# A two-layer attention and state-space kernel: y kept in PSUM, and the products of a step in another order

## The reference, cut to what matters

```
scores  = einsum('bcihn,bcjhn->bcijh', Cc, Bc) * Ldec * dtc      # Ldec = masked exp(cum_i - cum_j)
y_intra = einsum('bcijh,bcjhp->bcihp', scores, xc)
states  = einsum('bcjh,bcjhn,bcjhp->bchpn', dtc * dlast, Bc, xc)
y_inter = einsum('bcihn,bchpn->bcihp', Cc * exp(cum), prev)
y = y_intra + y_inter + Dp * x
```

## Time and profile before

| | us |
|---|---|
| median of 3 runs | 2378.64 |
| the profiled execution, its own time | 2379.2 |
| its span (first to last instruction) | 2377.5 |
| PE busy | 2070.7 (87%) |
| DVE busy | 1677.6 (71%) |
| ACT busy | 1429.3 (60%) |
| POOL busy | 1341.0 (56%) |
| mean granted TensorE clock | 0.948 of full speed |

### The profile page before, as it was taken

How to read it: one execution, slowest core, us unless ns; L and a number is a source line. 1 busy time by engine, 2 the same in 40 slices (tenths; PEclk the granted TensorE clock), 3 DMA queues, 4 the chain that set the end, 5 groups by cost and what they waited for, 6 DMA issues and landing times.

```text
span 2377.5 us, 33832 instructions
## 1 busy us (share of the span) xinstructions
PE 2070.7 (87%) x11288; PEld 1573.5 (66%) x11288; DVE 1677.6 (71%) x2927; ACT 1429.3 (60%) x2692; POOL 1341.0 (56%) x1233
## 2 busy tenths in 40 slices
PE   8899886888988888888888888888888888988768
PEld 4666664666666676667666766666666666766545
DVE  5777564667866787678667866786678667866756
ACT  1666416666666666666666667666666666666521
POOL 4545211556665666666656666656566656666561
PEclk9999987999999999999999999999999999999979
DMA  4000103222222222222222222222222222222200
GB/s 151 1 0 0 46 5 88 84 80 80 72 84 80 80 72 84 81 80 72 86 78 80 72 89 76 85 67 89 76 83 69 89 76 81 71 85 67 76 26 36
DMA packets 125707, 166.05 MB, mean 70 GB/s; under 512 B 37777, under 2 KB 88977, under 8 KB 121330
## 3 DMA queue, kind: packets, MB, share of 16 engines
q1 hardware_dynamic: 125554, 164.11, 21.3%
HBM read 159.88 MB, written 4.20 MB: 69 GB/s over the span
## 4 chain that ended last, share of the span: by engine, by line
ACT 26%; PE 23%; DVE 20%; issue 14%; POOL 5%; SPq 0%; DMA 0%; DVEq 0%; POOLq 0%; ACTq 0%
DVE conv L806 8%; ACT wq_t L1763 8%; PE p_gate_intra L102 7%; PE p_out L102 5%; ACT L1763 5%; ACT L1771 4%; DVE yT L1902 3%; PE p_mix L102 3%; ACT yT L1739 2%; ACT x_and_gate L1771 2%; ACT x_tokens L1732 2%; DVE p_inter_state L1989 2%; DVE x_skip L1994 2%; POOL wq_t L2123 2%; DVE state L1996 2%
## 5 line engine op out<-in xcount | busy, mean ns | idle before, releaser
L102 PE MATMUL p_out<-w_out,yT 128*128 128x512 f32 x1536 | 422.2, 427 | 117.5 <-DVE yT L1902 95.8
L102 PEld LDWEIGHTS p_out<-w_out,yT 128*128 128x128 f32 x1536 | 303.0, 203 | 223.9 <-DVE yT L1902 124.7
L102 PE MATMUL p_gate_intra<-x_high,w_gate 128*128 128x512 f32 x1024 | 369.9, 423 | 5.8 <-ACT x_and_gate L1771 4.6
L102 PE MATMUL p_mix<-x_high,w_x 128*128 128x512 f32 x1024 | 357.5, 411 | 16.4 <-DVE conv L806 15.0
L1902 DVE TENSOR_TENSOR yT<-y,yT 128x512 fp32r<-128x512 f32 x128 | 196.4, 1534 | 230.0 <-ACT yT L1739 229.4
L2123 POOL TENSOR_TENSOR wq_t<-wq_t,cb 128x1024 f32<-128x1024 f32 x128 | 331.1, 2587 | 4.9 <-ACT wq_t L1763 2.0
L2089 POOL TENSOR_TENSOR x_skip<-x_and_gate,group_skip 128x512 f32<-128x512 f32 x128 | 149.9, 1171 | 319.3 <-DVE p_gate_intra L1935 213.1
L1763 ACT ACTIVATE wq_t<-wq_t,minus_cum 128x128 f32<-128x128 f32 x1024 | 313.8, 389 | 8.2 <-DVE wq_t L1892 6.7
L806 DVE SCALAR_TENSOR_TENSOR conv<-p_mix,unit_small,conv 128x511 f32<-128x511 f32 (+2 forms) x384 | 286.3, 746 | 41.8 <-ACT conv L784 32.7
L794 ACT ACTIVATE x_and_gate<-conv 128x512 f32<-128x512 f32 x128 | 80.7, 631 | 382.0 <-DVE conv L806 381.4
L102 PEld LDWEIGHTS p_gate_intra<-x_high,w_gate 128*128 128x128 f32 x1024 | 204.2, 199 | 59.8 <-issue 16.0
(11 more groups left out here) (244 smaller groups left out, 4273.7 us busy)
## 6 DMA issues: line engine op xcount, KB each, us to landing
cum_all<-cum_rows SPq DMA_DIRECT2D x128, 512.0 KB, 3.8
exp_cum<-exp_rows SPq DMA_DIRECT2D x192, 128.0 KB, 3.2
w_staged<-in_w_gate SPq DMA_DIRECT2D x16, 1024.0 KB, 5.3
w_raw_tiles<-in_w_x SPq DMA_DIRECT2D x64, 256.0 KB, 3.2
w_staged<-in_w_out SPq DMA_DIRECT2D x16, 1024.0 KB, 4.9
w_raw_tiles<-in_w_bc SPq DMA_DIRECT2D x16, 256.0 KB, 5.3
x<-in_x SPq DMA_DIRECT2D x1, 2048.0 KB, 18.6
out<-x_and_gate SPq DMA_DIRECT2D x8, 256.0 KB, 2.0
```

The costliest lines, as they stand in the source:

```text
L102: last = pe.matmul(dst, left[a](k), right[b](k), start=k == 0 and n_ == 0, stop=stop and k == tiles - 1 and n_ == 2)
```

## The change

Four things are changed in the mixer, on all four compute engines.

1. y has no tile of its own any more. `make_y` multiplies in place in `p_intra` (PSUM), and `high_y`, `y_low_part` and `square_y` read it there. The scores' product of the next step, which writes `p_intra`, now waits for the squares (`sq_done`) in place of `y_done`; the squares wait for the low part (`y_split`).
2. On ACT the eight exponentials are cut into four and four, with `high_y` between them; before, it stood behind the gate's silu. In steps with c = 0 the silu of the gate stands earlier.
3. The squares' product goes into column 0 of `p_flip` in place of `p_inter`, and stands behind the scores' product of its step. It waits until `p_flip` has been emptied for the next step (`flip_out`), and the flips wait until its result has been read (`ms_read`). DVE reads the sum at the head of a step for the step before the last one (`older`), and `out_sum` follows the low part of y, for `older` too. `inverse_rms` on POOL stands right before decay times scores.
4. On PE the output product of the step before stands ahead of the channel projection. In a step with c = 0 the gate projection comes first. On POOL the skip part goes behind the two products with x (or, at c = 0 and 4, behind decay times scores).

The core of the diff:

```diff
-                def square_sums(g, k, dst):
+                def square_sums(g, k, flips):
                     s = step(g, k)
                     pe.wait_ge(sq_sum, s * 2 + 2)
+                    pe.wait_ge(flip_out, flips)
                     wait(pe, ms_read, s)
-                    pe.matmul(dst[:, 0:1], ysq[:, 0], one[:], start=True, stop=True).then_inc(ms_mm, 1)
+                    pe.matmul(p_flip[:, 0:1], ysq[:, 0], one[:], start=True, stop=True).then_inc(ms_mm, 1)
...
                     wait(pe, flip_out, step(g, k))
+                    wait(pe, ms_read, step(g, k) - (1 if c % CPS == 0 else 2))
...
                                 m.then_inc(inter_done, 1)
+                            if c < CHUNKS - 1:
+                                project_out(*before)
                             for i, e in convs:
                                 conv_event(i, e)
-                            if c < CHUNKS - 1:
-                                project_out(*before)
-                                pe.wait_ge(skip_sum, n_carries(g, k + 1))
-                                square_sums(*before, p_inter)
...
-                        wait(pe, y_done, s)
+                        wait(pe, sq_done, s)
...
                         if c == CHUNKS - 1:
                             project_out(*before)
-                            pe.wait_ge(skip_sum, n_carries(g, k + 1))
-                            square_sums(*before, p_inter)
+                        if before:
+                            square_sums(*before, s + 2 if (k + 1) % CPS else s + 1)
...
-                        decay_exps(s, k)
+                        decay_exps(s, k, 0, UNIT_HEADS // 2)
+                        high_y(*before)
+                        decay_exps(s, k, UNIT_HEADS // 2)
                         if c == CPS:
                             empty_x(g, k)
                         if s + AHEAD < TILES:
                             silu_gate(s)
-                        high_y(*before)
                         square_y(*before)
...
-                    dve.tensor_tensor(yT[:, 1], y[:], yT[:, 0].bitcast(F32), ALU.subtract).then_inc(y_split, 1)
+                    dve.tensor_tensor(yT[:, 1].rearrange("p j t -> p (j t)"), p_intra,
+                                      yT[:, 0].rearrange("p j t -> p (j t)").bitcast(F32), ALU.subtract).then_inc(y_split, 1)
...
-                    wait(dve, y_high, s)
-                    wait(dve, sq_done, s)
                     dve.wait_ge(y_sum, s + 1)
-                    dve.tensor_tensor(y[:], p_intra.rearrange("p (j t) -> p j t", t=P), chunk_of(SG, c // CPS, c % CPS),
-                                      ALU.mult).then_inc(y_done, 1)
+                    tiles = p_intra.rearrange("p (j t) -> p j t", t=P)
+                    dve.tensor_tensor(tiles, tiles, chunk_of(SG, c // CPS, c % CPS), ALU.mult).then_inc(y_done, 1)
...
+                        older = None if first and k < 2 else (g if k > 1 else g - 1, (k - 2) % STEPS)
+                        if older:
+                            mean_square(*older)
...
-                        if k == 0 and not first:
-                            out_sum(g - 1, STEPS - 2)
+                        if older and older[1] >= CHUNKS:
+                            out_sum(*older)
```

More of the change, by code:

```diff
@@ L1636, in group @@
                         if c == 0:
-                            if first and k == 0:
-                                project_gate(-3)
+                            project_gate(-3 if first and k == 0 else s)
                             conv_event(*convs[0])
@@ L1658, in group @@
                                 wait(pe, skip_sum, n_carries(g, k))
-                                wait(pe, ms_read, s - 1)
                                 for j in range(UT):
@@ L1701, in _ @@
                 project_out(GROUPS - 1, STEPS - 1)
[L1702 to L1703 removed]
+                square_sums(GROUPS - 1, STEPS - 1, GROUPS * STEPS)
                 pe.wait_ge(ms_read, GROUPS * STEPS)
@@ L1978, in group @@
                             y_low_part(*before)
-                        if c == 0 and not (first and k == 0):
-                            mean_square(before[0], before[1] - 1)
                         if c == 0:
                             arguments(s + 1, k + 1)
-                        if k == 0 and not first:
-                            out_sum(g - 1, STEPS - 2)
+                        if older and older[1] >= CHUNKS:
+                            out_sum(*older)
                         if carries(c):
@@ L2002, in group @@
                             arguments(s + 1, 0)
-                        summed = not (first and k == 0) and before[1] >= CHUNKS
                         def taps_of(events):
@@ L2022, in group @@
                             out_low_part(g * 2 + half, half)
-                        if not (first and k == 0):
-                            mean_square(*before)
                         if feeds(c):
@@ L2036, in group @@
                         make_y(g, k)
-                        if summed:
-                            out_sum(*before)
                         if last and k >= 2 * CHUNKS - 4:
@@ L2049, in _ @@
                 experts.low(dve, 1)
-                mean_square(GROUPS - 1, STEPS - 1, p_flip)
+                mean_square(GROUPS - 1, STEPS - 1)
                 for i in range(NORMED, CHUNKS):
@@ L2106, in group, with to_state @@
                             pool.wait_ge(group_done, g * 3 + 3)
-                        skip_part(g, k, first)
-                        if k == 0 and not first:
-                            inverse_rms(g - 1, STEPS - 2)
-                        pool.wait_ge(flip_out, s + 1)
-                        if feeds(c):
+                        older = (g if k > 1 else g - 1, (k - 2) % STEPS)
+                        def to_state():
                             wait(pool, st_done, n_feeds(g, k))
@@ L2133, in group @@
                             gate_low_part(g * 2 + half + 1, c - 3)
-                        if c < CHUNKS - 1 and not (first and k == 0) and before[1] >= CHUNKS:
-                            inverse_rms(*before)
                         if half and c in (1, 2) and not last:
```

63 lines of the change are left out of this document (38 added, 25 removed).

## The result

The changed kernel takes 2638.61 us (median of 4 runs, 2634.86 to 2642.34), the kernel before, on the same chip, 2377.61: a ratio of 1.1099 (95% interval 1.1078 to 1.112). It is 261 us slower; forecast were 216 us, with 2595 in a range of 2450 to 2700.

What follows compares the result with a forecast made beforehand. It took the period of ACT and DVE, 13.4 us an inner step, to bound the kernel. 2379.2 us plus 125 for longer steps plus 91 for the clock gave 2595, range 2450 to 2700.

Steps and rivals of the forecast that it cites:

- The loop: Inner mixer step through PE, ACT and DVE in series: 15.0 us in place of 13.4, PE idle 2.6 after the scores.
- the new wait, and the dear one: Squares' product behind the scores waits on PE until ACT empties p_flip for the next step; 2 to 3 us per inner step.
- ahead of the channel projection: Output product placed before the channel projection on PE: the last tap waits 2.9 us longer.
- E: The moment at which ACT has emptied p_flip for a step; the forecast counts a step from it to the next.
- The second wait: Steps 10 to 14: output product waits for out_sum behind POOL's late inverse root, until E + 6.5; projection 2.6 us later.
- steps 11 and 12: Two steps of a group in the list of step lengths, together put at 35.1 us without any loss of clock.
- The rival with this wait covered: POOL reaches the inverse root before PE needs the bank, and the clock holds: 2394 us, chance 0.07.
- The clock: PE runs partly at 1.2 GHz after idle stretches, 1.2 us lost each: 12 us a group, 91 us in all.
- The idle side: Longer steps without loss of clock: 16.4 us more in a group, 7.6 groups, 125 us.
- The rival without a loss of clock: New idle stretches on PE are too short to lower its clock: 2504 us, chance 0.19.
- The low part at 0.7: DVE's low part of y, with y now in PSUM, takes 0.7 us in place of a median 1.36.
- The faster rival: ACT empties p_flip before PE's scores end at E + 12.4: 125 us gained, 2254 us, chance 0.05.

Runs made afterwards that it cites:

- e_conv: Changed kernel with the output product put back behind the channel projection in steps 1 to 14, the rest as changed: 2228.86 us, 0.937 of the kernel before.
- e_psum_out: Kernel before with y in PSUM, high part between the exponentials and output product ahead of the channel projection, other orders as before: 2614.29 us, 1.0978.
- e_sq: Changed kernel with the squares' product one step later behind the gate projection in most steps, its sum read after the low part: 2643.01 us, 1.1121.
- e_fill: Changed kernel with eight more products, results unused, between scores and squares' product where that product waits for p_flip: 2549.96 us, 1.0728 of the kernel before.
- e_inv: Changed kernel with POOL's inverse root issued right behind the x_state product: 2537.67 us, 1.0671 of the kernel before.

## Why the prediction was right, and where it was not

- The loop. Right: PE, ACT and DVE in series, with PE idle after the scores. The inner step was put at 15.0 to 16.1 without the clock and is 16.3 to 17.1; the idle before L1598 was put at 2.6 and over 150 us in all, and is 2.6 and 237.8.
- What in it is dear. Wrong. The prediction said of the squares' product: "This is the new wait, and the dear one." `e_conv` left that product where it is and took 410 us off, `e_psum_out` was 9.8% slower than the kernel before without that wait, and `e_sq` took the wait away and the time stayed. The output product "ahead of the channel projection", to which the prediction gave 2.9 us, was the main cause. The sum was right, since it was made from E to E and not from the waits; its sentence on the parts was not. Had the change been its first three parts, a reader would have drawn the wrong sign from that sentence.
- The second wait. Right in mechanism, and only in part in place. It was forecast for steps 10 to 14. Averaged over the six middle groups it is 3.8 us in step 10 and 5.5 in 11 and 12 together, and in 13 and 14 PE doesn't wait for `out_sum` at all:

```profile
1451.77 3.04 PE L102 MATMUL p_out<-w_out,yT 128*128 128x512 f32 x12
```

  This is step 13 (E = 1444.8). The bank was free at 1451.4, E + 6.6 (6.5 forecast), but PE came still later, since its products from E on ran partly at the lower clock (0.83 on average in these two steps). So the length of 13 and 14 agrees, 20.4 each (20.1 forecast), partly by luck. In `e_fill`, where the clock is back there, the same steps show the forecast wait, 2.5 and 2.6 us. The worst sum is that of steps 11 and 12: 40.1 against 35.1. With the early root (`e_inv`) they take 34.9, so what was put too low is what the late root costs there. The rival with this wait covered takes 110 us off (2394 against 2504), and `e_inv` took 101; but these are not the same: the 110 are without the clock and for the whole wait, while `e_inv` left 58.6 us of it, and 62.8 of its 102 us of span are busy time. Also, that rival counts seven steps and 14.5 us, where the list has five steps of 2.6, 13.0.
- The clock. This is the term that fell shortest: 91 us. PE's busy time for the same products grew by 119.0. Two rows shown point to why: the gate behind a stop took 4.4 in place of 2.86, so a fall there costs 1.6, not 1.2; and the prediction left out the falls in front of the late root, "where PE waits anyhow", while the output product right behind such a stop takes 5.33 in place of 3.05. The idle side was put at 125 and grew by 141.8. 125 + 91 = 216 against 142 + 119 = 261. The groups say the same: 254.5 + 12 = 266.5 forecast, 273.6 measured; 5.0 of these 7.1 lie in steps 11 and 12. The rival without a loss of clock, 2504, falls by the page itself (0.896 against 0.948, 119.0 us), and `e_fill` ties the loss to the idle stretches.
- The low part at 0.7. Right (the line over the run; against the earlier trace rows):

```profile
L1901 DVE TENSOR_TENSOR yT<-p_gate_intra,yT 128x512 fp32r<-128x512 f32 x128 | 88.1, 688 | 70.4 <-ACT yT L1734 70.4
```

  It agrees with the rule of the Trainium skill ("SBUF — State Buffer", "Who interferes with whom") that the prediction named.
- The faster rival, that ACT empties `p_flip` before the scores end, missed by the 2.6 us that the prediction gave as its margin. It comes nearly true in `e_conv`, whose squares' product waits 0.38 and 1.09 us in the rows shown. That the gain was there behind one misplaced call, none of the rivals said; they took the four parts as one.

## What to carry to other kernels

Follow one step from a fixed event to the same event of the next step through all engines, and ask of each product whether it is in that loop; one that feeds only the far end (an output product) belongs behind one that feeds the next step, even if its input is ready first. The line where an engine waits is where slack collects, so test a cause by taking it away, and price each part of a change by itself before pricing the whole. When the wait that you took away comes back elsewhere, look at the steps one by one: some may have gained and others lost. Here a stop of PE often cost twice, the second time in the products behind it (in `e_inv` 62.8 us of busy time came back with 39.5 of idle time).

## What was not expected of the hardware

- More work made the kernel faster: 688 products with unused results, 182.2 us of PE, took 89 us off, by the clock (0.896 to 0.954). A stop of 2.65 us was followed by 0.68 and one of 2.64 by 1.00; what tells them apart is left open, and no run here tried to.
- The second instruction of `out_sum` reads three operands, two of them large tiles in SBUF. It went from a mean of 1.03 us before to 2.14, in an order that puts POOL's decay product (2.36 us) beside it (before, then after; busy, mean ns):

```profile
L1924 DVE SCALAR_TENSOR_TENSOR acc<-attn,inv_rms,acc 128x512 f32<-128x512 f32 x64 | 65.7, 1027 | 2.3
```

```profile
L1924 DVE SCALAR_TENSOR_TENSOR acc<-attn,inv_rms,acc 128x512 f32<-128x512 f32 x64 | 136.7, 2136 | 2.3
```

  The gain of 0.7 to 0.9 us at each low part was partly given back there. DVE's busy time still fell, from 1677.6 to 1638.7.
